# Gathers of 128 rows, one-hots by ScalarE in batches, and a second mix without GpSimd, in a graph network of three message passes

## The reference

```python
# one message pass (layer 0; layer 1 alike, its logits from per-node terms, 8 heads of 32)
xj = xl[src]                                             # gather of 50,000 rows
logits = leaky_relu(xj + xr[dst] + ee, 0.2) @ att
m = segment_max(logits, dst, n)
ex = exp(logits - m[dst])
out = segment_sum(xj * (ex / segment_sum(ex, dst, n)[dst])[:, None], dst, n) + b
# the mix of layer 1
q, k, v = split(xn @ W_qkv + b_qkv, 3); q = q - mean(q); k = k - mean(k)
q2, k2 = q * q, k * k
k2 = l2_normalize(k2 / (sum(k2, channels) + 1e-7), nodes)
q2 = l2_normalize(q2 / (sum(q2, channels) + 1e-7), channels)
attn = v + q2 @ (k2.T @ v) / sqrt(N)
out = attn @ W_out + b_out
```

## Time and profile before

| | us |
|---|---|
| median of 3 runs | 5197.01 (5194.62 to 5203.74) |
| the profiled execution | 5204.3 |
| its span in the trace | 5202.5 |
| message passes 1, 2, 3 (gathers start to end) | 1613 to 2290, 2537 to 3211, 3903 to 4593 |
| the mix of layer 1 (VectorE's first to last) | 4649 to 4808 |
| mean granted clock of TensorE | 0.855 of 2.4 GHz |

### The profile page before, as it was taken

How to read it: one execution, slowest core, us unless ns; L and a number is a source line. 1 busy time by engine, 2 the same in 40 slices (tenths; PEclk the granted TensorE clock), 3 DMA queues, 4 the chain that set the end, 5 groups by cost and what they waited for, 6 DMA issues and landing times. The chain is left out here.

```text
span 5202.5 us, 73734 instructions
## 1 busy us (share of the span) xinstructions
PE 4340.8 (83%) x21745; PEld 3584.4 (69%) x21746; DVE 2738.6 (53%) x8592; ACT 2171.7 (42%) x6651; POOL 2022.1 (39%) x1623
## 2 busy tenths in 40 slices
PE   9589999999995899988699998749936888878694
PEld 8478879788794777765577776438935666655694
DVE  2263452634523666764366666363355777766324
ACT  2243434434442666652366666122243333333222
POOL 0000000000004888840488885106618888833141
PEclk9789999999997999996899999659965666579697
DMA  5510000000005555530455553472267656620613
GB/s 141 145 52 10 18 10 1 18 10 18 1 21 124 126 126 125 125 88 19 98 125 127 129 125 83 93 219 68 63 146 151 136 135 135 134 67 25 202 36 87
DMA packets 364626, 463.24 MB, mean 89 GB/s; under 512 B 166429, under 2 KB 296743, under 8 KB 363790
## 3 DMA queue, kind: packets, MB, share of 16 engines
q1 hardware_dynamic: 172546, 258.16, 19.5%
q0 software_dynamic: 191744, 200.92, 17.5%
HBM read 396.61 MB, written 60.67 MB: 88 GB/s over the span
## 5 line engine op out<-in xcount | busy, mean ns | idle before, releaser
L656 POOL DMA_INDIRECT msg_rows<-tab_d,msg_cur x1296 | 1649.9, 1273 | 1762.8 <-DVE msg_cur L142 1368.7
L908 PE MATMUL msg_agp<-msg_rows,msg_oh 125*125 125x261 f32 (+2 forms) x2592 | 849.5, 457 | 14.3 <-DVE ga_acc L792 10.7
L908 PEld LDWEIGHTS msg_agp<-msg_rows,msg_oh 125*125 125x125 f32 x2592 | 549.0, 223 | 125.1 <-DVE ga_acc L792 18.2
L862 PE MATMUL msg_zp<-g_xr,msg_oht 127*125 x1728 | 544.3, 396 | 64.5 <-DVE msg_oht L696 64.2
L866 PE MATMUL msg_zp<-msg_rows,c_ident 125*125 125x256 f32 x1728 | 528.9, 387 | 81.9 <-DMA msg_rows<-tab_d,msg_cur 81.5
L701 DVE SCALAR_TENSOR_TENSOR msg_hid<-msg_zp,g_att 125x256 f32<-125x256 f32 x864 | 360.8, 420 | 334.3 <-PE msg_zp L866 329.5
L960 ACT ACTIVATE msg_dist<-c_iota,c_rel 125x125 f32<-125x125 f32 x1296 | 493.3, 387 | 49.7 <-PEq L3077 34.7
L964 ACT ACTIVATE msg_oh<-msg_dist,c_ones 125x125 f32<-125x125 f32 x1296 | 493.5, 387 | 0.0
L950 ACT ACTIVATE msg_ex<-msg_arg 125x16 f32<-125x16 f32 (+1 forms) x81 | 20.0, 247 | 984.9 <-DVE msg_delta L766 984.9
L866 PEld LDWEIGHTS msg_zp<-msg_rows,c_ident 125*125 125x125 f32 x1728 | 323.9, 190 | 153.7 <-DMA msg_rows<-tab_d,msg_cur 103.6
L792 DVE TENSOR_TENSOR gv_acc<-gv_acc,msg_agp 125x261 f32 (+1 forms) x864 | 364.4, 422 | 72.4 <-PE msg_agp L908 64.9
(11 more groups left out here) (552 smaller groups left out, 7221.1 us busy)
## 6 DMA issues: line engine op xcount, KB each, us to landing
msg_oht<-rel_d SPq DMA_DIRECT2D x81, 875.0 KB
msg_rows<-tab_d,msg_cur POOLq DMA_INDIRECT x1296, 3.9
pl_raw<-in_edge_attr SPq DMA_DIRECT2D x25, 448.0 KB
msg_pens<-pen_d SPq DMA_DIRECT2D x270, 31.2 KB
msg_oht<-rel_d SPq DMA_DIRECT2D x81, 101.6 KB
mix_w<-in_L_mix_W SPq DMA_DIRECT2D x8, 1024.0 KB
m0w_wr<-in_L_ffn_w SPq DMA_DIRECT2D x16, 512.0 KB
m0w_w2r<-in_L_ffn_w SPq DMA_DIRECT2D x16, 512.0 KB
```

The lines of the kernel that those rows point to most:

```text
L656: nc.gpsimd.indirect_dma_start(out=rows[:, q, k, :], out_offset=None, in_=table, in_offset=bass.IndirectOffsetOnAxis(ap=cur[:, q, k:k + 1] ...
L862: nc.tensor.matmul(z, hots, d_t, start=True, stop=False)
L908: nc.tensor.matmul(agp[:, sum_bank(u, k), 0:AW], oh[:, u % RB, k, :], rows[:, u % RB, k, 0:AW], start=True, stop=True).then_inc(summed.sem, 1)
```

## The change

There are five edits. (1) `ROWS = 128`: `rows`, `cur` and the source numbers have 128 partitions, so each gather fetches 128 rows; the last three go to partitions that nothing reads, and their source numbers are what the index tile holds there. (2) `edge_hots` writes Abs straight into `oh`, quarter by quarter, and one Relu works in place on a quarter (125 x 500): 16 + 4 instructions a group in the place of 32. It now waits for all sums of group g-3 first. (3) `node_hots` goes from VectorE's step 9 to the start of ScalarE's `body(j)`, still for group j+2, as Abs and Relu in place of 125 x 2000 each. (4) `rescale` with one head is a tensor_tensor with the factor broadcast, not a tensor_scalar. (5) `square_mix` uses no GpSimd: the sums of kk and k2 are VectorE's, three tiles behind `evict`; the 0/1 product (now L1847) goes to the loop's front, and the two additions to x (`base`: L1853, L1855) to the second phase, two tiles ahead of the output's addition.

```diff
@@ messages
-        rows = st.sb("rows", [P, RB, G, TW])
-        cur = st.sb("cur", [P, RB, G], I32)
+        rows_all = st.sb("rows", [ROWS, RB, G, TW])
+        rows = rows_all[0:P]
+        cur = st.sb("cur", [ROWS, RB, G], I32)
...
-  nc.gpsimd.indirect_dma_start(out=rows[:, q, k, :], out_offset=None, in_=table,
+  nc.gpsimd.indirect_dma_start(out=rows_all[:, q, k, :], out_offset=None, in_=table,
...
-  ch(nc.vector.tensor_scalar(a_t, a_t, fac[:, u % RB, 0:1], None, ALU.mult))
+  ch(nc.vector.tensor_tensor(a_t, a_t, fac[:, u % RB, 0:1].broadcast_to([P, W]), ALU.mult))
@@ VectorE's body, k == 9
-                            node_hots(j + 2, u + 2, i + (u + 2) // RB)
                             take_sources(j + RB, u)
@@ ScalarE, edge_hots(g, u)
-                    for k in range(G + 1):
-                        if k < G:
-                            nc.scalar.activation(dist[:, k % 4, :], c.iota[0:P, 0:P], ACT.Abs, scale=-1.0, bias=...).then_inc(dist_ready.sem, 1)
-                        if k == 0:
-                            continue
-                        act.wait_ge(dist_ready.sem, dist_ready.at(g * G + k))
-                        last = nc.scalar.activation(oh[:, u % RB, k - 1, :], dist[:, (k - 1) % 4, :], ACT.Relu, ...)
+                    if g >= RB:
+                        act.wait_ge(summed.sem, summed.at((g - RB + 1) * G))
+                    for b in range(5):
+                        if b < 4:
+                            for k in range(b * QS, (b + 1) * QS):
+                                last = nc.scalar.activation(oh[:, u % RB, k, :], c.iota[0:P, 0:P], ACT.Abs, ...)
+                            last.then_inc(dist_ready.sem, 1)
+                        if b == 0:
+                            continue
+                        act.wait_ge(dist_ready.sem, dist_ready.at(g * 4 + b))
+                        quarter = oh[:, u % RB, (b - 1) * QS:b * QS, :]
+                        last = nc.scalar.activation(quarter, quarter, ACT.Relu, ...)
+                def node_hots(g):
+                    act.wait_ge(hots_landed[g % RB].sem, hots_landed[g % RB].at((g // RB + 1) * hots_in))
+                    h = oht[0:P, g % RB]
+                    nc.scalar.activation(h, h, ACT.Abs, scale=-1.0, bias=c.part[0:P, 0:1]).then_inc(far_ready.sem, 1)
+                    act.wait_ge(far_ready.sem, far_ready.at(g + 1))
+                    nc.scalar.activation(h, h, ACT.Relu, scale=-1.0, bias=c.ones[0:P, 0:1]).then_inc(oht_ready.sem, 1)
@@ ScalarE's body(j, u)
+                    if j + 2 < NG:
+                        node_hots(j + 2)
                     weights(j, u)
@@ square_mix, GpSimd (the whole block goes)
-  nc.gpsimd.tensor_tensor(ksum[:], ksum[:], kk[:, t % R], ALU.add)
-  nc.gpsimd.tensor_tensor(x2[:, t], x2[:, t], shift[:], ALU.add)
-  nc.gpsimd.tensor_tensor(k2sum[:], k2sum[:], k2[:, t % R], ALU.add)
@@ square_mix, VectorE
+                def sums(t):
+                    ...
+                    nc.vector.tensor_tensor(ksum[:], ksum[:], kk[:, t % R], ALU.add)
+                    nc.vector.tensor_tensor(k2sum[:], k2sum[:], k2[:, t % R], ALU.add)
+                def base(t):
+                    ...
+                    nc.vector.tensor_tensor(row, row, acc4[:, t, :, 0:DH], ALU.add)
+                    nc.vector.tensor_tensor(x2[:, t], x2[:, t], shift[:], ALU.add)
...
-                for i in range(LP, NT + LP + 4):
+                for i in range(LP, NT + LP + 3):
...
-                    if LP + 4 <= i:
-                        closed(i - LP - 4)
+                    if LP + 3 <= i < NT + LP + 3:
+                        sums(i - LP - 3)
+                    if i < NT + LP:
+                        closed(i - LP)
```

More of the change, by code:

```diff
@@ L22 @@
 EVEN = 112
+ROWS = 128
 NT = N // P
@@ L413, in _ @@
                 dve.sem_inc(pens_ready.sem, 1)
-                take(1, c.src_s[:, 0:S], bank[0][0:P, 0:S])
+                take(1, c.src_s[0:P, 0:S], bank[0][0:P, 0:S])
                 take(2, c.last[:], bank[1][0:P, 0:S])
@@ L613, in messages @@
         dist_ready = st.sem("dist_ready")
+        far_ready = st.sem("far_ready")
         z_ready = st.sem("z_ready")
@@ L983, in body @@
                         edge_hots(j + 1, u + 1)
+                node_hots(0)
                 edge_hots(0, 0)
+                node_hots(1)
                 body(0, 0)
@@ L1574, in square_mix @@
         xk = [st.ps(f"xk{j}", [128, D]) for j in range(2)]
[L1575 removed]
+        order = st.sem("order")
         w_in, v_in, small_in = st.sem("w_in"), st.sem("v_in"), st.sem("small_in")
@@ L1819, in _ @@
                 ch(nc.vector.reciprocal(zero[:], d))
+                ch(nc.vector.tensor_tensor(shift[:], bq[:, 2], bias[:], ALU.add))
                 def evict(t):
@@ L1843, in queries @@
                     nc.vector.tensor_scalar(qh[:, t % R], sq[:, t % R, 0], rec[:, t, 0:1], qn[:, t:t + 1], ALU.mult, ALU.mult).then_inc(q_ready.sem, 1)
+                def sums(t):
+                    dve.wait_ge(kk_ready.sem, kk_ready.at(t + 1))
+                    dve.wait_ge(k2_ready.sem, k2_ready.at(t + 1))
+                    if t >= 1:
+                        dve.wait_ge(k2_summed.sem, k2_summed.at(t))
+                    nc.vector.tensor_tensor(ksum[:], ksum[:], kk[:, t % R], ALU.add).then_inc(kk_summed.sem, 1)
+                    nc.vector.tensor_tensor(k2sum[:], k2sum[:], k2[:, t % R], ALU.add).then_inc(k2_summed.sem, 1)
                 def closed(t):
-                    ch(nc.vector.tensor_tensor(acc4[:, t, :, 0:DH], acc4[:, t, :, 0:DH], zero[:, t].unsqueeze(2).broadcast_to([P, HEADS, DH]), ALU.mult))
-                    dve.wait_ge(based.sem, based.at(t + 1))
+                    nc.vector.tensor_tensor(acc4[:, t, :, 0:DH], acc4[:, t, :, 0:DH], zero[:, t].unsqueeze(2).broadcast_to([P, HEADS, DH]), ALU.mult).then_inc(closed_ready.sem, 1)
+                def base(t):
                     row = x2[:, t].rearrange("p (h f) -> p h f", h=HEADS)
-                    nc.vector.tensor_tensor(row, row, acc4[:, t, :, 0:DH], ALU.add).then_inc(x2_ready.sem, 1)
-                for i in range(LP, NT + LP + 4):
+                    dve.wait_ge(x_in[t // U].sem, x_in[t // U].at(32))
+                    nc.vector.tensor_tensor(row, row, acc4[:, t, :, 0:DH], ALU.add).then_inc(closed_ready.sem, 1)
+                    dve.wait_ge(closed_ready.sem, closed_ready.at(NT + t + 1))
+                    nc.vector.tensor_tensor(x2[:, t], x2[:, t], shift[:], ALU.add).then_inc(x2_ready.sem, 1)
+                for i in range(LP, NT + LP + 3):
                     if i < NT + LP:
@@ L1863, in _ @@
                 nc.vector.tensor_scalar_mul(kn[:], kn[:], ROOT).then_inc(kn_ready.sem, 1)
-                dve.wait_ge(x2_ready.sem, x2_ready.at(NT))
+                dve.wait_ge(bvo_ready.sem, bvo_ready.at(1))
+                ch(nc.vector.tensor_tensor(shift[:], shift[:], bvo[:], ALU.add))
+                dve.wait_ge(closed_ready.sem, closed_ready.at(NT))
+                for t in range(2):
+                    base(t)
                 for t in range(NT):
+                    if t + 2 < NT:
+                        base(t + 2)
+                    dve.wait_ge(x2_ready.sem, x2_ready.at(t + 1))
                     dve.wait_ge(out_done.sem, out_done.at(t + 1))
```

38 lines of the change are left out of this document (6 added, 32 removed).

## The result

The changed kernel took 5514.57 us (median of 4 runs, 5492.37 to 5524.55), the kernel before beside it 5195.82 (5175.43 to 5203.74): ratio 1.0614, 95% interval 1.0568 to 1.066, so 6.1% slower, where 5098 us and a gain had been forecast. The number of that chip is not on record. On chips 12 and 10 the same kernel later took 5067 and 5065 us, 2.5% faster than before; one more execution on chip 10 took 13,640 us at a mean clock of 0.487, which none of the other 138 executions on record comes near, and since it has no trace and no explanation it is left out of these figures. Both sides are shown here, the slow one first.

What follows compares the result with a forecast made beforehand. GpSimd's gathers were taken to bound passes 1 and 2, with TensorE next. Against 5204.3 us profiled, -39 - 34 - 4 - 5 - 17 = -99 gave 5105, or 5098 us as a median; range 5060 to 5150.

Steps and rivals of the forecast that it cites:

- gather of 128 rows: GpSimd's gathers: 1.10 us each at 128 rows, between 1.00 and 1.25, against 1.214 at 125 rows.
- pass 1, first gather to last argument: First message pass: groups fall from 25.25 to 23.7 us, -39, plus a quicker start, -4 for passes 1 and 2.
- pass 2: Second message pass: groups fall from 24.93 to TensorE's 23.57 us, -34, plus its share of the quicker starts.
- pass 3: Third message pass: consumers are slower than GpSimd, so quicker gathers count at the start alone, -5 us.
- mix and after: Second mix: a first-phase tile falls from 4.06 to 3.2 us; second-phase additions hidden; together -17 (-10 to -22).
- TensorE as the next bound: Passes 1 and 2: once gathers are quick enough, groups run at TensorE's own rate, 23.57 us.
- ScalarE: Moved one-hot work, 2.5 to 4.0 us a group, hides in 9.72 us idle before L950; 5.7 left at worst; cost 0.
- rival E: Pass 3 speeds up too: without L696 VectorE brings logits 1.3 us a group earlier, -35 more, 5063 us; chance 0.10.
- A: Rival on gathers: 128 rows cost what 125 do, 1.21 us, total 5138 us; chance 0.20.
- C: Rival on gathers: the price per row holds, 1.25 us at 128 rows, total 5164 us; chance 0.10.
- D: Slower rival on gathers: GpSimd's price climbs in steps of row count, about 1.33 us, total 5253 us; chance 0.05.
- The slower rival: The same as D: dearer gathers of 128 rows slow all three passes, +56 us; chance 0.05.

Runs made afterwards that it cites:

- h3: The changed kernel, unchanged, six executions on chip 5: 5517.42 us, ratio 1.0604 to the kernel before.
- h1: The changed kernel, unchanged, six executions on chip 12: 5067.2 us, ratio 0.9744 to the kernel before.
- e3: The kernel before with the changed second mix (`square_mix`) and nothing else, chip 12: 5180.82 us, ratio 0.9944.
- f1: The kernel before with gathers of 128 rows and node_hots on ScalarE, chip 1: 5084.56 us, ratio 0.9772.
- f2: The kernel before with gathers of 128 rows and the edge one-hots in batches, chip 1: 5105.22 us, ratio 0.9803.
- f3: The kernel before with gathers of 128 rows and the rescaling with two SBUF inputs, chip 1: 5092.8 us, ratio 0.9784.
- f4: The kernel before with gathers of 128 rows and the changed second mix, chip 1: 5082.83 us, ratio 0.9778.
- g3: The changed kernel with node_hots on VectorE as before, chip 10: 5081.24 us, ratio 0.9766 to the kernel before.
- k1: Passes 1 and 3 of the kernel before with gathers of 128 rows, pass 2 and second mix as changed, chip 3: 5080.72 us, ratio 0.9773.
- g1: The kernel before with gathers of 128 rows, node_hots on ScalarE and edge one-hots in batches, chip 10: 5092.02 us, ratio 0.9786.
- g2: The changed kernel with the second mix of before, chip 10: 5085.95 us, ratio 0.9783 to the kernel before.
- e1: The changed kernel with gathers of 125 rows again, chip 12: 5140.79 us, ratio 0.9861 to the kernel before.

## Why the prediction was wrong

**The step that failed** is one that the working took for granted and gave no rival: that when GpSimd's gathers get quicker the groups run at TensorE's own 23.57 us. In the result, and on chip 5, they run at 29.0 to 29.7 (first 25 distances of passes 1 and 2), since TensorE's increments arrive late. Shown: that they are late, by 4.3 us in nearly every group and by up to 41 us at a pass's start; that all ten executions of the changed kernel in the result and on chip 5 are slow, and both that have a trace show the late increments, while those on chips 10 and 12 show none; that the time is lost in the three passes; that the new rescaling isn't needed for it. Argued: that the gathers do it, and those of 128 rows in particular. For the gathers speaks that the same increment is late behind a row of them and on time in the three groups without them, and that at the start of a pass 40 us of stops fall in a stretch with hardly anything else at work. For the 128 rows speaks only that the kernel before, with 125, ran at 5195 and 5201 us beside the slow ones. Against its being proved: no kernel with 128 rows alone, and none with 125 or 126 rows and the other edits, came onto such a chip; the stop up to 1679.56 outlasts the last gather by 5 us; and on the other chips gathers as dense hold nothing. One rival is untested: the slow traces also lack half of the semaphore records of the passes, and no run tells whether the recording takes part in the holding. The DMA packets don't differ between the chips (32 of 4176 bytes and 16 of 4 bytes per gather; in the first pass 0.263 and 0.260 us for one of 4176 bytes, h3 and h1), so the data's transfer is not slower. Open stays what differs in the chip.

**The terms of the sum** can be held against g0, the changed kernel on chip 10, where nothing is held. Windows of its first and third pass, then its argument operations and gathers, and how long a gather takes to land, before and in g0:

```profile
1596.60:2260.00 663.40, 622.39 (x2933) 499.44 (x2933) 436.48 (x1940) 477.47 (x1081) 412.15 (x432) 0.98 0.51 131
...
3791.70:4500.00 708.30, 573.77 (x2069) 436.39 (x2070) 462.30 (x1209) 307.59 (x649) 440.61 (x432) 0.64 0.52 134
```

```profile
L758 DVE TENSOR_TENSOR msg_arg<-msg_lg,msg_m x27: 162/165/172, 1637.6 to 2248.7; 125x16 f32<-125x16 f32 x27
...
L758 DVE TENSOR_TENSOR msg_arg<-msg_lg,msg_m x27: 162/165/172, 2510.5 to 3118.2; 125x16 f32<-125x16 f32 x27
...
L758 DVE TENSOR_TENSOR msg_arg<-msg_lg,msg_m x27: 279/280/289, 3825.1 to 4483.5; 125x128 f32<-125x128 f32 x27
```

```profile
L658 POOL DMA_INDIRECT msg_rows<-tab_d,msg_cur x432: 940/946/1087, 1596.6 to 2219.7; - x144
```

```profile
DMA to landing us min/median/max: 3.8/3.9/12.7
```

```profile
DMA to landing us min/median/max: 2.7/2.8/3.8
```

| term, us | forecast | measured (before to g0) |
|---|---|---|
| gather of 128 rows | 1.10 (1.00 to 1.25) | 0.946 |
| group, pass 1 / pass 2 (median) | 23.7 / 23.57 | 23.71 / 23.54 |
| pass 1, first gather to last argument | -41 | 699.9 to 652.1: -47.8 |
| pass 2 | -36 | 694.3 to 649.3: -45.0 |
| pass 3 | -5 | 714.9 to 691.8: -23.1 |
| mix and after | -17 | 584.2 to 565.1: -19.1 |
| sum | -99 | -135 |

The two traces are 154 us apart, since g0's first gather also comes 16.6 us earlier, in stages that the change doesn't touch; by the executions beside each other g0 gains 138 us and h1 134. So even where nothing is held the gain was forecast a quarter too small, by the starts of the passes and by pass 3. Such times, 5065 and 5067, lie inside the stated range.

*Gathers:* right in kind, cheaper than either bound; that made the starts shorter. A first argument comes 41.1 us after the first gather in place of 49.4: 16 gathers of 0.27 less are 4.3 us, and a landing of 2.8 in place of 3.9 gives 1.1. The other 2.9 are mostly of the other edits: with 128 rows alone (e2) it is 43.4. The forecast had -2 per pass. Four sizes are now measured: 108 rows 1.00 (of another table), 125 rows 1.21, 126 rows 0.997, 128 rows 0.946. So the price does not fall with the rows; 125 stands out. By the rule of the Trainium skill, "DMA: Bandwidth & Descriptors" ("Why a DMA increments its semaphore by 16 and not by 1"), as I apply it, these counts are cut into 12, 5, 14 and 16 shares, of 9, 25, 9 and 8 rows; the four prices follow the rows a share. That this is the cause was not tried by itself.

*TensorE as the next bound:* right to 0.03 us a group. *ScalarE:* a wide activation takes 1.95 us, and idle time before the weights is still there:

```profile
2030.55 1.95 ACT L971 ACTIVATE msg_oht<-msg_oht,c_part 125x2000 f32<-125x2000 f32 x1
...
2040.50 0.22 ACT L945 ACTIVATE msg_ex<-msg_arg 125x16 f32<-125x16 f32 x1 [6.01 <-DVE msg_delta L764]
```

6.0 us of 9.72 are left, the worst case of the forecast was 5.7. The cover held, cost 0.

*The mix,* one tile of g0:

```profile
4570.21 0.68 DVE L1818 TENSOR_TENSOR sq_qk<-sq_pq,sq_bq 125x512 f32<-125x512 f32 x1
...
4571.95 0.41 DVE L1836 TENSOR_SCALAR ga_ee<-sq_sq,sq_rec,sq_qn 125x256 f32<-125x256 f32 x1
...
4572.62 0.42 DVE L1844 TENSOR_TENSOR sq_k2sum<-sq_k2sum,ga_ee 125x256 f32<-125x256 f32 x1
...
4573.29 0.68 DVE L1818 TENSOR_TENSOR sq_qk<-sq_pq,sq_bq 125x512 f32<-125x512 f32 x1
```

3.08 us a tile (forecast 3.13 by parts, 3.2 taken), no stalls: e3 alone gives 0.9944, 26.6 us below the 5207.41 beside it; the trace of the whole has -19.1. The second phase hid the additions.

*Pass 3:* mis-sized. It was to gain at the start alone; the start gave 7.3 (40.8 to 33.5), the groups 15.7 more. Argument operations of e2 and of f1, third pass:

```profile
L762 DVE TENSOR_TENSOR msg_arg<-msg_lg,msg_m x27: 279/280/289, 3848.6 to 4520.8; 125x128 f32<-125x128 f32 x27
```

```profile
L759 DVE TENSOR_TENSOR msg_arg<-msg_lg,msg_m x27: 280/280/286, 3836.0 to 4496.7; 125x128 f32<-125x128 f32 x27
```

672.2 us with L696 on VectorE and 660.7 without it: 11.5 us are L696's. The other traces with 128 rows and nothing held agree: 668 to 673 us in six with L696 on VectorE (e2, f2, f3, f4, g3, k1), 655 to 663 in five without it (f1, g0, g1, g2, h1). That is rival E at a third of its price, 0.4 us a group and not 1.3. Gathers beside the scaling (now L771) were still slowed, as in the earlier trace rows; in g0's third pass 97 of the 117 that overlap with it are over 0.1 us above the median, and 5 of the 287 that don't:

```profile
4006.16 1.25 DVE L771 TENSOR_TENSOR msg_rows<-msg_rows,msg_ex 125x1056 f32<-125x1056 f32 x1
...
4006.76 1.47 POOL L658 DMA_INDIRECT msg_rows<-tab_d,msg_cur  x1 [0.30 <-issue]
```

*Rivals:* A was right for e1 (5140.79 measured, 5138 worked out), C and D never came up (C's first term, 25 x 0.41, is -10 and not -11; its time stays). The slower rival had the right sign for the result and chip 5 by a wrong mechanism: it let the gather's price rise, and its price fell.

## What to carry to other kernels

When an engine's stream gets denser, ask not only which engine bounds next but whether anything shares a path with that stream; here quicker gathers, alone or with the other edits, were a gain of 2 to 2.5% on four chips (1, 3, 10, 12) and, with the other edits, a loss of 6% in the result and on chip 5. A result that no single edit explains is to be measured on a second chip before it is taken apart: the changed kernel again, ahead of its parts, would have told this sooner. And variants meant to find the cause are worth something only where the effect is there. Where it must hold everywhere, the changed kernel with 125 rows (0.9861 on chip 12) keeps the spacing of gathers of the kernel before, but it too was not seen on a chip that holds increments.

## What the runs showed of the hardware that was not expected

- Semaphore increments of one engine can be held back, here TensorE's by 4.3 us in 24 of 27 groups and by 5.5 to 41.5 us at the start of a pass, and then arrive in a burst, while VectorE's pass at once. It came in 12 of 12 executions on chip 5 and shows in no trace of chips 1, 3, 10 and 12.
- The profile shows it only indirectly: idle time put down to "remote" or "issue", with the producer's instruction long done, and half of the semaphore records of a pass missing (4951 on record in place of 10,853). A stop whose named reason lies in the past is the sign to look for.
- An indirect gather of 128 rows is cheaper for GpSimd than one of 108 from another table (0.946 and 1.00 us), and lands 1.1 us sooner than one of 125 (2.8 and 3.9).
- A VectorE tensor_tensor with both inputs in the core's own memory slows the gathers beside it: 97 of the 117 gathers that overlap with L771 in g0's third pass, by up to 1.09 us.
